# Routing masks laid out with the choice/block pair innermost, written-out number rows, and an earlier store of the last rows

## The reference, cut to what matters

```python
t = to_tokens(x)                            # 2048 x 256
S = sigmoid(layernorm(t) @ Wg)              # 8 experts
G, I = top_k(S, 2)                          # two choices per token
h = gelu(einsum('nd,edf->enf', xt, W1) + b1[:, None, :])     # 256 -> 1024
y = einsum('enf,efd->end', h, W2) + b2[:, None, :]           # 1024 -> 256
out = einsum('ne,end->nd', combine, y)      # combine holds G at the chosen experts
result = from_tokens(t + out)
```

## Time and profile before

| what | value |
|---|---|
| median of 3 runs (lowest, highest) | 341.78 us (341.45, 342.4) |
| profiled execution, span from first to last instruction | 341.7 us |
| PE, DVE, ACT, POOL busy | 305.1, 249.4, 182.0, 153.3 us |
| DVE from line 1319 to the end of the masks | 104.35 to 111.72 us |
| first gather issued | 113.33 us |
| first product of step 0, of step 3 | 119.21, 134.72 us |
| last line 530 issued | 333.73 us |

### The profile page before, as it was taken

One profiled execution on the slowest core, in us unless ns is written; L12 is line 12 of the kernel. 1 busy time (PEld: TensorE's weight loads), 2 busy tenths in 40 slices (PEclk: granted clock), 3 DMA queues, 4 the chain that ended last, 5 costly groups with the idle time before them and its releaser, 6 DMA issues.

```text
span 341.7 us, 8716 instructions
## 1 busy us (share of the span) xinstructions
PE 305.1 (89%) x3066; PEld 231.2 (68%) x3066; DVE 249.4 (73%) x596; ACT 182.0 (53%) x509; POOL 153.3 (45%) x162
## 2 busy tenths in 40 slices
PE   8999899999610788999999999999999999999960
PEld 8777633567410386888888888888888888877730
DVE  3896978669899689979797978888756564665430
ACT  3547487616723355676767676666534445354310
POOL 2233542347520630665655554665455453635331
PEclk9999999999965699999999999999999999999995
DMA  7500000002379383788787878784353433333210
GB/s 215 171 3 1 2 0 1 0 31 88 115 238 287 87 269 109 213 207 215 199 198 196 204 196 197 195 206 79 67 87 62 87 63 69 64 56 64 52 19 2
DMA packets 36202, 39.42 MB, mean 115 GB/s; under 512 B 8416, under 2 KB 32832, under 8 KB 36160
## 3 DMA queue, kind: packets, MB, share of 16 engines
q1 hardware_dynamic: 29184, 29.56, 29.2%
q0 software_dynamic: 6976, 9.31, 16.1%
HBM read 29.74 MB, written 9.11 MB: 114 GB/s over the span
## 4 chain that ended last, share of the span: by engine, by line
PE 67%; DVE 14%; DMA 10%; issue 3%; ACT 2%; POOLq 0%; POOL 0%; SPq 0%; ACTq 0%
PE ps L912 15%; PE ps L897 8%; PE ps L901 8%; PE ps L899 8%; DMA out<-fb,idx 8%; PE ps L913 8%; PE ps L756 5%; PE ps L737 3%; DMA xt<-x_tok 2%; PE ps L851 2%; PE ps L765 2%; PE ps L769 2%; PE ps L772 2%; PE ps L845 2%; PE ps L804 1%
## 5 line engine op out<-in xcount | busy, mean ns | idle before, releaser
L674 ACT ACTIVATE fb<-ps,b1t 128x128 f32<-128x128 f32 (+7 forms) x312 | 82.0, 376 | 83.6 <-issue 80.8
L912 PE MATMUL ps<-wt,fb 128*128 x312 | 117.0, 379 | 0.0
L897 PE MATMUL ps<-fb,wt 128*128 128x128 f16 (+7 forms) x624 | 114.3, 214 | 2.7 <-DVE fb L1357 2.7
L901 PE MATMUL ps<-fb,wt 128*128 128x128 f16 (+7 forms) x624 | 114.3, 214 | 0.9 <-issue 0.9
L899 PE MATMUL ps<-fb,wt 128*128 128x128 f16 (+7 forms) x624 | 114.3, 214 | 0.0
L530 POOL DMA_INDIRECT out<-fb,idx x39 | 62.6, 1604 | 96.4 <-DVE s2c L1400 62.6
L913 PE MATMUL ps<-wt,fb 128*128 x312 | 85.0, 272 | 0.0
L897 PEld LDWEIGHTS ps<-fb,wt 128*128 x624 | 61.0, 98 | 33.6 <-issue 3.8
L899 PEld LDWEIGHTS ps<-fb,wt 128*128 x624 | 60.4, 98 | 3.3
L520 POOL DMA_INDIRECT fb<-xn_rows,idx x39 | 49.2, 1261 | 26.3 <-DVE idx L1335 12.8
L901 PEld LDWEIGHTS ps<-fb,wt 128*128 x624 | 60.4, 98 | 0.4 <-issue 0.4
(11 more groups left out here) (209 smaller groups left out, 397.1 us busy)
## 6 DMA issues: line engine op xcount, KB each, us to landing
wt<-w SPq DMA_DIRECT2D x32, 512.0 KB
b2t<-b SPq DMA_DIRECT2D x39, 128.0 KB
out<-xt SPq DMA_DIRECT2D x8, 256.0 KB, 2.1
xn_rows<-wt SPq DMA_DIRECT2D x8, 256.0 KB, 3.3
xt<-x_tok SPq DMA_DIRECT2D x3, 512.0 KB, 6.9
b1t<-params SPq DMA_DIRECT2D x39, 4.0 KB
fb<-xn_rows,idx POOLq DMA_INDIRECT x39
out<-fb,idx POOLq DMA_INDIRECT x39
```

The lines of the kernel that those rows point to most:

```text
L674: a = nc.scalar.activation(hid[:, s, f * P:f * P + ROWS[n]], h_ps(s)[:, f * P:f * P + ROWS[n]], ACT.Gelu_apprx_tanh, bias=b1t[:, n % NBIAS ...
L897: pe.matmul(dst, hi, xT[:, s, c * P:c * P + rows], start=(c == 0 and f % 4 == 0), stop=False, skip_group_check=True)
L901: m = pe.matmul(dst, lo, xT[:, s, c * P:c * P + rows], start=False, stop=(c == DC - 1), skip_group_check=True)
L912: pe.matmul(y_ps(s), hhi[:, s, f * P:(f + 1) * P], w, start=(f == 0), stop=False)
```

## The change: what it does

- `hot` and `pay` are laid out with the 32 pairs innermost: `hot` is row by pair, `pay` is version by tile by pair.
- The numbers 0 to 127 and 0 to 39 are no longer read from `c16` with a repeat; POOL writes them out in full at the start with two `iota` instructions, `iota_wide` (128 x 16 numbers a partition) and `tiles_wide` (40 x 32), in space of the fourth expert's weights. DVE waits for them (`wide_set`) where it waited for `c16`.
- The comparisons and products of lines 1319, 1323, 1326 and 1362 run over the new layout: the same element counts, with the pair's number repeated along an outer axis.
- PE's `table` reads `hot[:, :, k]` and `pay[:, v:v + n, :, k]`: 128 or 40 elements that lie 32 elements (64 bytes) apart.
- SP stores the last rows of `xn` after two of the four weight quarters, not after all four.
- ACT splits two quarters, runs the sigmoid and the gelu of one element, and then splits the other two.

```diff
-        hot = place(3, 0, 2 * NBLK * P).rearrange("p (q r) -> p q r", r=P)
+        hot = place(3, 0, 2 * NBLK * P).rearrange("p (r q) -> p r q", q=2 * NBLK)
+        wide = 2 * NBLK * P
+        iota_wide = place(3, wide, P * NBLK).rearrange("p (r k) -> p r k", k=NBLK)
+        tiles_wide = place(3, wide + P * NBLK, TCOL * 2 * NBLK).rearrange("p (i q) -> p i q", q=2 * NBLK)
...
-        pay = late[:, 0:2560].bitcast(F16).rearrange("p (q v i) -> p q v i", v=4, i=TCOL)
+        pay = late[:, 0:2560].bitcast(F16).rearrange("p (v i q) -> p v i q", v=4, i=TCOL)
...
             sp.wait_ge(perm_done, 1)
-            for h in range(NSTG):
+            for h in range(DC):
                 load(h)
             rows_out(B - 1)
+            for h in range(DC, NSTG):
+                load(h)
...
+            nc.gpsimd.iota(iota_wide, [[1, P], [0, NBLK]], base=0, channel_multiplier=0,
+                           allow_small_or_imprecise_dtypes=True)
+            nc.gpsimd.iota(tiles_wide, [[1, TCOL], [0, 2 * NBLK]], base=0, channel_multiplier=0,
+                           allow_small_or_imprecise_dtypes=True).then_inc(wide_set, 1)
...
-            for h in range(QUARTERS_FIRST):
+            for h in range(DC):
                 split_hi(h)
             act.wait_ge(logit_done, 2)
             nc.scalar.activation(sgl[:, :, :], lg[:, :, :], ACT.Sigmoid, scale=1.0 / XS).then_inc(sigl_done, 1)
             nc.scalar.activation(scrap[:, :], eps_c, ACT.Gelu_apprx_tanh)
+            for h in range(DC, QUARTERS_FIRST):
+                split_hi(h)
...
-                    m = pe.matmul(ps[:, bank, 0:n * TCOL], hot[:, k, :], pay[:, k, v:v + n, :].rearrange("p v i -> p (v i)"),
+                    m = pe.matmul(ps[:, bank, 0:n * TCOL].rearrange("p (v i) -> p v i", i=TCOL), hot[:, :, k], pay[:, v:v + n, :, k],
                                   start=(k == 0), stop=(k == 2 * NBLK - 1))
...
-            dve.wait_ge(c16_in, 16)
-            iota16, tiles16 = c16[:, C16["iota"]], c16[:, C16["tiles"]]
-            over_tiles = lambda x, n: x.unsqueeze(2).broadcast_to([P, n, TCOL])
+            over_tiles = lambda x, n: x.unsqueeze(1).broadcast_to([P, TCOL, n])
...
-            v.tensor_tensor(out=pay[:, :, 0, :], in0=tiles16.unsqueeze(1).broadcast_to([P, 2 * NBLK, TCOL]),
-                            in1=over_tiles(flat(place16[:, 1]), 2 * NBLK), op=ALU.is_equal).then_inc(pay_done, 1)
+            dve.wait_ge(wide_set, 1)
+            v.tensor_tensor(out=pay[:, 0], in0=tiles_wide, in1=over_tiles(flat(place16[:, 1]), 2 * NBLK),
+                            op=ALU.is_equal).then_inc(pay_done, 1)
...
-                v.tensor_tensor(out=hot[:, half, :], in0=iota16.unsqueeze(1).broadcast_to([P, NBLK, P]),
-                                in1=place16[:, 0, a].unsqueeze(2).broadcast_to([P, NBLK, P]), op=ALU.is_equal)
+                v.tensor_tensor(out=hot[:, :, half], in0=iota_wide,
+                                in1=place16[:, 0, a].unsqueeze(1).broadcast_to([P, P, NBLK]), op=ALU.is_equal)
                 dve.wait_ge(pay_done, 1)
-                v.tensor_tensor(out=pay[:, half, 1, :], in0=pay[:, half, 0, :], in1=over_tiles(tok16[:, :], NBLK),
+                v.tensor_tensor(out=pay[:, 1, :, half], in0=pay[:, 0, :, half], in1=over_tiles(tok16[:, :], NBLK),
                                 op=ALU.mult).then_inc(hot_done, 1)
...
-                    ins = v.tensor_tensor(out=pay[:, :, n, :], in0=pay[:, :, 0, :],
+                    ins = v.tensor_tensor(out=pay[:, n], in0=pay[:, 0],
                                           in1=over_tiles(flat(place16[:, n]), 2 * NBLK), op=ALU.mult)
```

More of the change, by code:

```diff
@@ L304, in build @@
         sel_done = sem("sel_done")
+        wide_set = sem("wide_set")
         prefix_mm = sem("prefix_mm")
```

## The result

The changed kernel takes **343.53 us** (median of 22 runs) against 341.88 us for the kernel before (22 runs) on the same chip: ratio **1.0040, 95% interval 1.0027 to 1.0053**. A gain of 4.0 us was forecast; by the ratio there is a loss of 1.4 us (1.65 between the two medians). Of forecast and rivals only rival 4 had a loss that can be measured.

The account below looks back on a forecast made before the run. DVE was taken to bound the mask stretch, PE the steps after it. Step 0 earlier by 3.1 us plus 0.84 us less gap before step 3 gave 3.96 off 341.78: 337.8 us, range 336.5 to 340.2.

Parts of the forecast that it names:

- rival 4: PE's strided weight loads run one behind the other at 191 ns or more; slower, 344.2 us; 5%.
- Strided reading by PE (a loss): PE's table products read elements 64 bytes apart; claimed losses of 0.3 and 0.6 us, bounded by nothing and 2.4 and 4.8.
- p1: Strided reading's cost on the second 16 products of the first table, before step 0; 0.3 us, at most 2.4.
- p2: Strided reading's cost on all 32 products of table(2), before step 3; 0.6 us, at most 4.8.
- rival 1: Strided reading doubles PE's product spacing, costing 0.7 us before step 0 and 1.3 before step 3; 338.9 us; 20%.
- Masks: DVE's comparisons before the first table run at 0.53 ns an element instead of 1.04; 3.42 us saved.
- rival 3: DVE's comparisons stay at 1.04 ns an element, so the change does not do what it says; 342.1 us; 7%.
- gate_pay: DVE's two 1,280-element instructions ahead of step 3 (L1362) get shorter; 1.32 us saved.
- G: How much of PE's gap before step 3 closes; 1.44 - 0.6 = 0.84 us.
- S: How much earlier step 0 starts; 3.42 - 0.3 = 3.1 us.
- The store: SP's earlier store of the last rows lands 1.2 us or more before idx; without it S would be lost.
- Rival 2: The store or the gather holds step 0, leaving 1.0 us gained there and 0.84 before step 3; 339.9 us; 12%.

Follow-up runs that it names:

- e8: Changed kernel with PE operands at a 4-byte step and biases of steps 1 to 3 issued after the first gather landed; 339.06 us, ratio 0.9895 to before.
- e2: Changed kernel with hot left in its old layout, so only PE's moving operand (pay) is strided; 344.65 us, ratio 1.0072 to before.
- e7: Changed kernel with only the two choices innermost, so PE reads both operands at a 4-byte step; 339.80 us, ratio 0.9939 to before.
- e10: Changed kernel with two blocks' pairs innermost, so PE reads both operands at an 8-byte step; 341.45 us in one run, not compared.
- e9: Changed kernel with four blocks' pairs innermost, so PE reads both operands at a 16-byte step; 343.92 us in one run, not compared.
- e5: Changed kernel with the old order on SP and ACT, the store again behind all four quarters; 343.51 us, ratio 1.0034 to before.
- e3: Changed kernel with the old mask layout, contiguous for PE, each pair's number written twice, no iota; 340.95 us, ratio 0.9956 to before.
- e6: Contiguous PE operands, pair numbers written twice, biases of steps 1 to 3 issued after the first gather landed; 338.47 us (four runs), ratio 0.9875 to before.
- e11: Changed kernel with PE at a 4-byte step and later biases between and behind the next expert's weight quarters; 339.29 us, ratio 0.9911 to before.
- e1: Changed kernel with pay left in its old layout, so only PE's stationary operand (hot) is strided; 340.91 us, ratio 0.9965 to before.

## Why the prediction was wrong

**The step that failed: "Strided reading by PE (a loss)".** It put p1 = 0.3 and p2 = 0.6 us, "half the spacing again", near the lower end of its bounds, because the row behind the upper end was one of f32 weights and these are f16. Measured: p2 = 4.94 - 1.31 = 3.63. For p1, DVE's wait for table(1) is 1.44 us in the changed kernel and 0.61 in e8, where PE reads at 4 bytes: 0.8. Both lie within their bounds, p1 a third and p2 three quarters of the way up, and the sign that the prediction named, 32 products at 2.6 us or above, is there. Two things misled. The step looked only at weight loads for its upper end, while e2 shows that most of the price is the moving operand's; and the rule weighed in rival 1, a price for every 16-byte line, fits what e7, e10 and e9 measured, and was given 0.7 and 1.3 us only because nothing in the trace sized it. Rival 4 named the right size of product (143 ns decides; table(2) has 154) and came out at 344.2, near the measured time. That was luck: it put the whole price on the weight loads and had no fall of the clock. It had 5%.

**A term that was not in the sum.** Behind the strided stretch the granted clock fell to 0.50, which cost 1.6 us of step 3 (windows above; 166.6 against 168.2 from step 3 to the store). The prediction's last sentence said that the forecast falls if the time after step 3 isn't the same; it wasn't. The same fall follows table(2) in e2, e5 and e9 (4.5 to 5.0 us of it); in the other ten profiles (1.3 to 2.6 us) the clock stays at 1.00 there. So the fall goes with the long strided table(2); why the clock falls no run shows. A full busy share alone doesn't explain it, as the earlier trace rows has 25 us of that at 1.00. Nor is such a stretch the only occasion: in e10 the clock fell in the first products of step 0, whose operands no edit touches, after PE had stood idle for 0.99 and 1.04 us, and stayed at 0.50 for some 3.4 us:

```profile
116.66 0.23 PE L913 MATMUL ps<-fb,wt 128*128 128x128 f16 x1 [1.04 <-DVE fb L1372]
...
116.79 0.31 PE L917 MATMUL ps<-fb,wt 128*128 128x128 f16 x1
116.90 0.31 PE L913 MATMUL ps<-fb,wt 128*128 128x128 f16 x1
```

**By its other steps:**

- Masks (3.42 saved): right, 3.47; 0.53 ns an element was the rate, and rival 3 is out.
- gate_pay (1.32): right, 1.24. But G, forecast 0.84, became a loss: in the second profile of before DVE's wait ahead of step 3 was 1.29 us as in the earlier trace rows; that went, and 3.63 came. (The gap was also 1.33 us and not the 1.44 of the sum: without a wait step 3 starts 1.27 us after table(2) does, as in e3.)
- S (3.1): 2.4 to 2.8. p1 took 0.5 more than forecast, and PE waits 0.54 us for the gather, within the 0.7 allowed.
- The store: it landed 4.9 us after its issue at 101.40, 3 us before idx. Right in sign, but "without it S would be lost" was too strong, as e5 shows: 0.6 us. Rival 2 lived on in another form, the gather's own landing behind the biases, which decides only once PE's stride is out of the way (e3, e7).
- Quarters three and four: covered. ACT splits them at 109.42 without a wait and is done at 111.4.
- iota: hidden. 2.47 and 1.38 us, 3.85 in all, a little under the lower bound of 4.0; POOL still waits for its first copy:

```profile
2.33 2.47 POOL L459 IOTA wt<- 128x2048 f16 x1
4.77 1.38 POOL L461 IOTA wt<- 128x1280 f16 x1
6.87 0.40 POOL L465 COPY wt<-cst 128x256 f32<-128x256 f32 x1 [0.73 <-DMA cst<-const]
```

- The clock row: the prediction saw four low slices "around 102 to 136 us". The earlier trace rows has three, from 94 to 120 us; before the change the clock stood at 1.00 through step 3.
- The reference: the profile of before was a long execution (above), with a gap of 0.9 us before the last product of step 0 that the second profile lacks. The sum was one of differences, so this moved its base, not its size.

Without the strided step the sum would still have been too large for this order of transfers: e3 and e7, whose PE operands cost nothing, gain 1.5 and 2.1 us by their ratios. There the 0.7 us allowed for the gather were too few, as PE waits 1.27 and 1.79 us for it; with the biases moved the gain is 3.0 to 4.3.

## What to carry to other kernels

A layout is paid for by every reader: when an axis is moved innermost for DVE, work out at how many bytes PE will then step. Here four f16 elements of one product to 16 bytes cost nothing, and two already doubled the product's time. For DVE's fast rate two adjacent elements were enough here, so the cheapest layout is the one that disturbs PE least. Where a cost has no row and one end of its bounds turns the verdict, that end deserves more than 5%.

## What the runs showed of the hardware

- PE's moving operand (f16) at 64 bytes: 1.7 ns a column (e2, the same at either clock level). With the other operand strided too, 32 products of 80 columns take 42 ns each at 4 bytes, where it costs nothing, 80 at 8, 155 at 16 and 154 at 64, or 1.9 ns for each 16-byte piece entered. The stationary operand at 64 bytes alone: 2.17 us for 32 products, 68 ns each.
- The granted clock fell from 1.00 to 0.50 at the end of 4.9 us in which the profile shows PE busy without a gap, on 32 strided products (e2, e5 and e9 likewise). In e10 it fell to 0.50 behind two idle stretches of 1 us.
- Comparing f16 pairs with each number written twice (2,048 elements in 1.22 us) is as fast as with the whole axis contiguous (1.22 us).
- The first gather on POOL's queue landed in 3.75 to 3.8 us with the biases out of its way (e6, e8, e11) and in 4.7 to 6.25 us beside them (the changed kernel, e1, e9, e3, e7, e10), though they are small (4 and 128 KB each).
